# Probabilities stationary in self-attention's value products, Tanh time scales and another startup order in a decoder layer

## The reference, cut to what matters

```python
q_in = linear(x, Wq_w, Wq_b)            # then a width-3 convolution, and a projection of both
Q = linear(concat(q_in, conv1d(q_in)), qproj_w, qproj_b)     # the same for K; V = linear(x)
tau   = sigmoid(conv1d(gelu(conv1d(x, tau1_w)), tau2_w))     # per head and query
delta = sigmoid(conv1d(gelu(conv1d(x, del1_w)), del2_w))     # per head and key
scores = Q @ K.T / sqrt(8) * tau + delta
out = softmax(scores) @ V               # [heads, 128 queries, 8]
x = x + linear(out, out_w, out_b)
```

## Time and profile before

| | |
|---|---|
| median of 3 runs | 305.3 us |
| the profiled execution | 305.65 us, of which 303.8 us from its first to its last instruction |
| PE, ScalarE, VectorE, GpSimd busy | 95%, 63%, 75%, 61% of the span |
| PE weight loads (PEld) busy | 68% of the span |
| mean granted PE clock | 0.987 of full |

### The profile page before, as it was taken

One profiled execution on the slowest core, in us unless ns is written; L12 is line 12 of the kernel. 1 busy time (PEld: TensorE's weight loads), 2 busy tenths in 40 slices (PEclk: granted clock), 3 DMA queues, 4 the chain that ended last, 5 costly groups with the idle time before them and its releaser, 6 DMA issues.

```text
span 303.8 us, 5436 instructions
## 1 busy us (share of the span) xinstructions
PE 288.5 (95%) x1721; PEld 206.5 (68%) x1721; DVE 227.5 (75%) x511; ACT 192.7 (63%) x353; POOL 185.1 (61%) x258
## 2 busy tenths in 40 slices
PE   8999599999999999899879999999999999999995
PEld 3754476667655665466664788888888888888883
DVE  3695599789959886989796559788965766676664
ACT  2787647887784667466752797666655555555553
POOL 8430044087807880876167699999975666666661
PEclk9999789999999999999999999999999999999999
DMA  7703635447477233250000637866444344343321
GB/s 269 230 2 48 204 77 135 109 109 258 110 192 145 62 94 107 62 152 16 0 2 18 185 118 200 216 191 200 122 108 138 112 168 123 128 137 128 118 69 35
DMA packets 30636, 37.18 MB, mean 122 GB/s; under 512 B 5136, under 2 KB 19856, under 8 KB 30608
## 3 DMA queue, kind: packets, MB, share of 16 engines
q1 hardware_dynamic: 30608, 36.84, 43.3%
HBM read 28.43 MB, written 3.93 MB: 107 GB/s over the span
## 4 chain that ended last, share of the span: by engine, by line
PE 79%; DVE 14%; ACT 4%; issue 2%; ACTq 0%; DVEq 0%
PE bank L484 54%; PE bank L863 5%; PE bank L865 5%; PE bank L864 5%; PE bank L669 2%; DVE rawmax L1282 2%; PE bank L644 2%; PE bank L687 2%; DVE conv L1221 2%; DVE conv L1219 2%; PE bank L656 1%; PE bank L692 1%; PE bank L653 1%; PE bank L490 1%; DVE tauT L1349 1%
## 5 line engine op out<-in xcount | busy, mean ns | idle before, releaser
L1846 POOL TENSOR_TENSOR qbd<-vs,qbd 128x512 fp32r<-128x512 f32 x65 | 83.6, 1289 | 33.3 <-ACT qbd L1160 33.2
L484 PE MATMUL bank<-khl,stacks 128*128 128x512 f32 x396 | 101.5, 392 | 1.9 <-DVE vs L1643 1.9
L484 PEld LDWEIGHTS bank<-khl,stacks 128*128 128x128 f32 x396 | 73.5, 188 | 18.7 <-issue 3.7
L1674 DVE TENSOR_TENSOR conv<-bank,conv 128x512 f32<-128x512 f32 x60 | 41.5, 691 | 31.5 <-ACT bank L1124 28.3
L1124 ACT ACTIVATE bank<-bank 128x512 f32<-128x512 f32 x61 | 35.5, 582 | 44.0 <-PE bank L484 44.0
L1282 DVE TENSOR_REDUCE rawmax<-bank 128x4 f32<-128x512 f32 x64 | 43.2, 683 | 8.8 <-PE bank L484 7.8
L484 PE MATMUL bank<-stacks 128*128 128x512 f32 x96 | 42.8, 498 | 4.4 <-DVE stacks L1258 3.3
L1160 ACT ACTIVATE qbd<-vs 128x512 fp32r<-128x512 f32 x65 | 40.6, 625 | 7.1 <-DVE vs L1651 4.6
L1682 DVE TENSOR_TENSOR vs<-conv,bank 128x512 f32<-128x512 f32 x61 | 41.9, 687 | 2.1
L1048 ACT ACTIVATE conv<-bank 128x512 f32<-128x512 f32 x64 | 35.1, 596 | 6.3 <-PE bank L484 5.4
L1810 POOL TENSOR_TENSOR stacks<-ring,stacks 128x384 fp32r<-128x384 f32 x33 | 33.6, 1017 | 1.4
(11 more groups left out here) (238 smaller groups left out, 439.6 us busy)
## 6 DMA issues: line engine op xcount, KB each, us to landing
conv<-coefficient_rows SPq DMA_DIRECT2D x122, 128.0 KB, 2.9
ring<-w SPq DMA_DIRECT2D x33, 192.0 KB, 3.6
stacks<-stacks SPq DMA_DIRECT2D x68, 64.0 KB, 2.1
split_rows<-stacks SPq DMA_DIRECT2D x6, 256.0 KB, 2.6
stacks<-split_rows SPq DMA_DIRECT2D x16, 96.0 KB
split_rows<-khl SPq DMA_DIRECT2D x3, 512.0 KB, 4.3
stacks<-split_rows SPq DMA_DIRECT2D x8, 192.0 KB
pa<-pack_a SPq DMA_DIRECT2D x1, 706.0 KB, 5.4
```

Of the source, the lines that this page charges most:

```text
L484: return pe.matmul(out, lhsT, rhs, start=start, stop=stop)
L1674: dve.tensor_tensor(out, gate, spread[:, n % ROWS, :, :], ALU.mult).then_inc(gate_scaled, 1)
L1846: pool.tensor_tensor(hlo[:, n % 4, :].rearrange("p (b t) -> p b t", b=4), hx[n % 4], hhi[:, n % 4, :].bitcast(F32).rearrange("p (b t) -> p ...
```

## The change

1. Time scales: ScalarE computes Tanh of half the argument, with half the bias (tau_half, made on GpSimd), and VectorE makes the Sigmoid of it, 0.5 t + 0.5, before the query product.
2. Startup order: PE turns the first inputs before it sums the queries' bias, and sums the keys' bias after the first query convolution; ScalarE copies the keys' composed taps after the first tap, and runs the high keys' first half and the first time scales before the last late Gelu; VectorE adds the folded biases between tau's and delta's taps and makes the first low keys before the query products.
3. Value products of self-attention: the probabilities (128 keys x 128 queries) are stationary and the values (128 keys x 9) moving; the result has the queries on partitions and lies in bank 4 as 16 x 9 columns (attended). copy_o and turn_out run for cross-attention alone; norm reads bank 4 directly in self-attention.
4. Query quadrants: in self-attention ScalarE copies all four, VectorE none. Waits follow these changes.

```diff
+        attended = bank[4][:, 0:H * (DK + 1)].rearrange("p (h c) -> p h c", h=H)
...
             compose(0)
+            turn_inputs(0, 0, bank[0])
             sum_bias(0, "qp2T", "cqb", "bq")
-            turn_inputs(0, 0, bank[0])
             compose(1)
-            sum_bias(1, "kp2T", "ckb", "bk")
             turn_inputs(0, 1, bank[1])
...
                 convolve(0, convq, c, bank[5 + c]).then_inc(q_done, 1)
+                if c == 0:
+                    sum_bias(1, "kp2T", "ckb", "bk")
...
             def turn_max(s):
                 wait(pe, qbd_high, s)
-                wait(pe, qbd_ready, s)
+                wait(pe, qbd_ready, s - B)
...
             def pv(s, g):
                 i = G * s + g
                 pe.wait_ge(exped, i + 1)
-                if g == 0:
-                    wait(pe, o_copied, s)
+                if g == 0 and s <= B:
+                    wait(pe, normed, s)
+                elif g == 0:
+                    pe.wait_ge(o_copied, s - B)
                 for j in range(J):
-                    last = mm(bank[4][32 * j:32 * j + DK + 1, P * g:P * g + P], vs[s // B][:, s % B, J * g + j, :],
-                              probs[:, i % 8, j, :])
+                    h = J * g + j
+                    if s < B:
+                        last = mm(attended[:, h, :], probs[:, i % 8, j, :], vs[0][:, s, h, :])
+                    else:
+                        last = mm(bank[4][32 * j:32 * j + DK + 1, P * g:P * g + P], vs[1][:, s % B, h, :], probs[:, i % 8, j, :])
...
             def turn_on(s):
                 pe.wait_ge(normed, s + 1)
+                wait(pe, residual, s)
...
-                if s >= 1 and making is None:
+                if s > B and making is None:
                     turn_out(s - 1)
...
             copy_inputs(0, 0, 0)
-            copy_composed(1, convk)
             copy_inputs(0, 1, 1)
...
+            def time_scales(c):
                 act.wait_ge(tau_done, c + 1)
-                act.activation(half(tauT, c), four(3 + c), ACT.Sigmoid, bias=A("tau2b")).then_inc(tau_ready, 1)
+                act.activation(half(tauT, c), four(3 + c), ACT.Tanh, scale=0.5, bias=tau_half[:, :]).then_inc(tau_ready, 1)
...
+            first_tap(0, 0, "tau1", "tau1b")
+            copy_composed(1, convk)
+            first_tap(0, 1, "tau1", "tau1b")
...
+            first_tap(1, 0, "del1", "del1b")
+            early_gelu(0)
+            first_tap(1, 1, "del1", "del1b")
+            early_gelu(1)
+            fill_keys(1)
+            fill_keys(2)
+            late_gelu(0)
+            fill_keys(3)
             act.wait_ge(bias_folded, 2)
+            act.wait_ge(k_done, 1)
+            high_keys(0, 0, 7, foldb[:, 1:2])
+            act.wait_ge(halves_ready, 2)
+            time_scales(0)
+            late_gelu(1)
+            time_scales(1)
             high_queries(0)
             high_queries(1)
-            act.wait_ge(k_done, 1)
-            high_keys(0, 0, 7, foldb[:, 1:2])
             act.wait_ge(k_done, 2)
             high_keys(0, 1, 0, foldb[:, 1:2])
...
-                for j in range(J - 1 if s < B else 2):
+                for j in range(J if s < B else 2):
...
-                if s >= 1:
+                if s > B:
                     copy_o(s - 1)
...
+            low_keys(0, 0, 7, foldb[:, 1:2])
             for c in range(2):
                 dve.wait_ge(q_done, c + 1)
                 dve.wait_ge(tau_ready, c + 1)
+                dve.tensor_scalar(half(tauT, c), half(tauT, c), 0.5, 0.5, ALU.mult, ALU.add).then_inc(tau_scaled, 1)
+                dve.wait_ge(tau_scaled, c + 1)
...
             low_queries(0, 0)
-            low_keys(0, 0, 7, foldb[:, 1:2])
+            low_keys(0, 1, 0, foldb[:, 1:2])
             low_queries(0, 1)
-            low_keys(0, 1, 0, foldb[:, 1:2])
...
             def norm(s):
-                dve.wait_ge(o_turned, s + 1)
-                o = bank[6][:, :].rearrange("p (h c) -> p h c", h=H)
+                if s < B:
+                    dve.wait_ge(pv_done, G * s + G)
+                else:
+                    dve.wait_ge(o_turned, s - B + 1)
+                o = attended if s < B else bank[6][:, :].rearrange("p (h c) -> p h c", h=H)
...
-                if s < STEPS:
+                if B <= s < STEPS:
                     queries_with_max(s)
```

More of the change, by code:

```diff
@@ L101, in decoder_layer @@
         natural = qin[:, :, :].rearrange("p b t -> p (b t)")[:, 4 * P:6 * P].rearrange("p (n i) -> p n i", n=2)
-        negbias = sb("negbias", [P, 2])
+        small = sb("small", [P, 3])
+        negbias, tau_half = small[:, 0:2], small[:, 2:3]
         foldb = sb("foldb", [P, 2])
@@ L208, in decoder_layer @@
         tau_ready = sem("tau_ready")
+        tau_scaled = sem("tau_scaled")
         delta_done = sem("delta_done")
@@ L664, in scoresT @@
                     pe.wait_ge(qbd_high, s + 1)
-                    pe.wait_ge(qbd_ready, s + 1)
+                    wait(pe, qbd_ready, s - B + 1)
                 wait(pe, exped, i - 1)
@@ L807, in _ @@
                     scoresT(s, 3)
-                if making is not None:
+                if making is not None and s > B:
                     turn_out(s - 1)
@@ L849, in _ @@
             pe.wait_ge(exped, G * STEPS)
-            pe.wait_ge(o_copied, STEPS)
+            pe.wait_ge(o_copied, STEPS - B)
             products(0)
@@ L975, in _, with high_queries, late_gelu @@
             act.wait_ge(ld_a, 16)
[L976 to L990, removed]
+            def high_queries(c):
+                act.wait_ge(q_ready, c + 1)
+                act.activation(half(qhl[:, 0, :, :], c), half(qc, c), ACT.Copy).then_inc(qhi_ready, 1)
+            def late_gelu(r):
                 act.wait_ge(conv_done, 3 + r)
@@ L993, in _, with early_gelu @@
                     act.activation(gelu_half(r, b), conv[:, 2 + r, b:b + 4, :], ACT.Gelu).then_inc(gelu_done, 1)
-            for c in range(2):
+            def early_gelu(r):
+                act.wait_ge(conv_done, r + 1)
+                act.activation(conv[:, r, :, :], conv[:, r, :, :], ACT.Gelu).then_inc(gelu_done, 1)
+            def time_scales(c):
                 act.wait_ge(tau_done, c + 1)
-                act.activation(half(tauT, c), four(3 + c), ACT.Sigmoid, bias=A("tau2b")).then_inc(tau_ready, 1)
-            def high_queries(c):
-                act.wait_ge(q_ready, c + 1)
-                act.activation(half(qhl[:, 0, :, :], c), half(qc, c), ACT.Copy).then_inc(qhi_ready, 1)
-            act.wait_ge(bias_folded, 2)
+                act.activation(half(tauT, c), four(3 + c), ACT.Tanh, scale=0.5, bias=tau_half[:, :]).then_inc(tau_ready, 1)
+            t0 = cols_a["tau2T"][0]
+            act.wait_ge(xT_copied, 2)
+            first_tap(0, 0, "tau1", "tau1b")
+            copy_composed(1, convk)
+            first_tap(0, 1, "tau1", "tau1b")
+            act.activation(tau2r[:, :, :, :].rearrange("p r h d -> p (r h) d"),
+                           pa[:, t0:t0 + 2 * H].unsqueeze(2).broadcast_to([P, 2 * H, DK]), ACT.Copy).then_inc(const_ready, 1)
+            first_tap(1, 0, "del1", "del1b")
[6 more added lines that the diff above has]
+            fill_keys(3)
+            act.wait_ge(bias_folded, 2)
+            act.wait_ge(k_done, 1)
[4 more added lines that the diff above has]
+            time_scales(1)
             high_queries(0)
             high_queries(1)
-            act.wait_ge(k_done, 1)
-            high_keys(0, 0, 7, foldb[:, 1:2])
             act.wait_ge(k_done, 2)
@@ L1034, in copy_o @@
                 act.wait_ge(pv_done, G * s + G)
-                wait(act, o_turned, s)
+                wait(act, o_turned, s - B)
                 act.activation(oT[:, :, :].rearrange("p g t -> p (g t)"), bank[4][:, :], ACT.Copy)\
@@ L1209, in _ @@
             last.then_inc(picks_ready, 1)
-            dve.wait_ge(bias_summed, 2)
-            for n, bias in enumerate(("qpb", "kpb")):
-                dve.tensor_tensor(foldb[:, n:n + 1], bank[4][:, n:n + 1], A(bias), ALU.add).then_inc(bias_folded, 1)
             def later_taps(n, w):
@@ L1226, in _ @@
             later_taps(0, "tau1")
+            dve.wait_ge(bias_summed, 2)
+            for n, bias in enumerate(("qpb", "kpb")):
+                dve.tensor_tensor(foldb[:, n:n + 1], bank[4][:, n:n + 1], A(bias), ALU.add).then_inc(bias_folded, 1)
             later_taps(1, "del1")
@@ L1241, in values, with low_keys @@
                 last.then_inc(v_copied, 1)
+            def low_keys(n, c, b, bias):
+                dve.wait_ge(khi_ready, 2 * n + c + 1)
+                dve.scalar_tensor_tensor(out=half(khl[n][:, 1, :, :], c), in0=four(b), scalar=bias,
+                                         in1=half(khl[n][:, 0, :, :], c).bitcast(F32), op0=ALU.add,
+                                         op1=ALU.subtract).then_inc(klo_ready, 1)
+            low_keys(0, 0, 7, foldb[:, 1:2])
             for c in range(2):
@@ L1295, in queries_with_max @@
                 wait(dve, scoredT, G * (s - 1))
```

(6 more changed lines are left out.)

2 lines of the change are left out of this document (1 added, 1 removed).

## The result

The changed kernel takes 339.94 us, median of 4 runs (338.24 to 343.9), against 305.48 for the kernel before on the same chip: ratio 1.1112 [1.1069, 1.1155]. The forecast was 325.6 with a range of 313 to 334: the direction was right, the size too small by some 14 us, and the time lies outside the range. The profiled execution is the one of 338.24 us.

A forecast was written before the change was run, and what follows sets the result against it. Startup was taken as bound by a VectorE-ScalarE chain, self-attention steps by PE's queue, then exponentials, last maximum and normalisation. Sum: 305.65 - 3.5 (startup) + 16.8 (value products, transposes) + 7 (clock) = 325.95, or 325.6 on the median's footing; range 313 to 334.

The forecast's parts named there:

- the clock: Self-attention steps: about one stretch of PE at half rate in each of seven steps, +7 us, bounds 0 and +13.
- Value products and transposes: Self-attention steps: longer products +2.26 us, removed transposes credited 0.16; +2.1 each step, +16.8 over eight.
- Query quadrants: Self-attention: ScalarE's fourth copy adds 0.60 us, hidden at no cost; with short products it would stand on the path.
- New waits: Self-attention: value products waiting for the previous norm to read bank 4, and turn_on's wait on the residual, cost nothing.
- Startup up to the stacking: Startup: PE starts stacking at 31.4 instead of 33.58, and a full clock shortens its products; startup -3.5 us.
- SP must keep up ... no loss: Startup transfers: eight end at 31.9, six more take 3.08 us to 35.0, when step 1's blocks leave without loss.
- The clock stays full: Rival for the self-attention steps: no half-rate stretches, total 318.95 us (315 to 321); chance 0.22.
- Tanh not under Gelu's table: Rival for the startup: three table loads instead of one, about +2 in place of -3.5, total 331.5 us; chance 0.08.
- Loads beside each other: Rival for value products: 128x128 tile loads overlap, products cost as before, total 298 us; decides from 0.06 us an instruction; chance 0.08.

The follow-up runs named there:

- the keys first: Startup part of the change alone on the kernel before, with SP issuing step 1's keys ahead of the split queries' rows: 301.75 us, ratio 0.9862.
- 63-column run: The changed kernel with each self-attention value product streaming its 9 value columns seven times over, same loads: 320.56 us, ratio 1.0486.

## Why the prediction was wrong, by its own steps

**The step that failed: the clock.** The mechanism was named, and its price was nearly right; how long the clock stays down was wrong. The prediction had "about one stretch at half rate in each of seven steps", each of 3.41 us at 1.0 us apiece, +7. Measured: 17.4 us for 48 us at half rate, that is 14 of the prediction's stretches, at 1.24 us each. The clock did not fall more often than forecast: it was at half six times in the steps, from 54.2, 61.0, 88.3, 95.1, 105.4 and 115.6, for 3.4, 20.5, 3.4, 6.8, 6.8 and 6.8 us. Only those of steps 1 and 4 (54.2 and 88.3) are as short as forecast. In steps 5, 6 and 7 the clock fell already in the second block of value products and came back only with the end of the step. The forecast also assumed that a step's score half would bring the clock back before the next step's products. It didn't always: from within step 2 to the end of step 3 it stayed at half for one stretch of 20.5 us, in which PE was idle for 0.32 us, while the stretch behind it is at full clock:

```profile
61.01:81.49 20.48, 20.16 (x72) 16.67 (x73) 6.75 (x18) 7.40 (x15) 8.91 (x12) 0.50 0.18 41
81.49:88.32 6.83, 6.61 (x50) 5.70 (x49) 3.86 (x12) 3.44 (x6) 2.58 (x13) 1.00 0.70 253
```

The price per stretch was reckoned for the score half, 1.0 us. On the product blocks half rate takes 7.12 us for 3.81. Even the bound of +13 (1.7 us in each of eight steps) allowed one such stretch a step, and so was no bound. What brings the clock down is shown by the runs with 9, 27, 63 and 126 columns behind the same loads: 48, 24, 0 and 0 us at half rate in the steps. At half rate the loads slow down too (3.77 us of them become 7.02 in the product blocks above). Why the clock returns when it does was not tried and stays open. The row that the term was read from the earlier trace rows was thin evidence: with the keys first, the same delta products run at 36.01 and 37.59, and the clock stays full to 49 us.

**Value products and transposes: right as a sum.** 3.81 us was forecast for the block at full clock, and 3.81 measured in step 1. With the clock full throughout, the steps cost 16.5 us more; the forecast was 16.8. Step by step it is less exact: in the 63-column run the steps grew by 1.39 to 2.58 us, where 2.1 was forecast for each. In its step 3 the score half grew by 0.45 us (2.88 to 3.33), where 0.16 was credited for the transposes, so part of the agreement is luck. The delta products, loads of the same tile with 16 columns streamed, were the right row to price it by.

**Query quadrants: right, with its condition.** Hidden in the changed kernel, and at full clock too (in step 3 of the 63-column run the copies end at 67.67, and PE asks for them at 69.25). Without the longer products to hide them, and with copy_o kept, they cost 1.65 us over the eight steps, 1.04 of it in step 3 (5.30 to 6.34) and 0.50 in step 6 (6.09 to 6.59). The prediction's 0.6 for that case is not reached in most steps; in step 3 the copy itself is 0.44.

**New waits: right.** At full clock the 63-column run has no gap before its products. Of the idle time of PE that the trace notes in its steps, most is for the exponentials (1.1 us) and the maxima (1.0), which the kernel before waits for as well (0.3 each); none of it is a new wait.

**Startup up to the stacking: right.** The stacking starts at 31.17, where 31.4 was forecast; the rescaling takes 0.43 (0.42 was taken); at full clock the stacking is 1.21 us shorter (1.3 was forecast). At the last of the key products before the wait the kernel is 3.62 us ahead (38.53 against 42.15), the forecast's 3.5.

**Startup, "SP must keep up ... no loss": wrong, by 2 us.** The prediction put the six split-row transfers down at 3.08 us because they had taken that before. But there SP had been free for 3.13 us ahead of them (from 30.40, the end of the eight, to 33.53); now they follow the eight directly. They took 4.93, and step 1's keys left at 37.32 instead of 35.0. PE's wait of 2.15 us followed, which left 1.75 us of the gain (41.77 against 43.52), and with 6.78 us at half rate (40.57 to 47.35) 1.25 us were left at turn_max(1). Keys first brought them back: 3.88 us at that mark.

With these the sum closes on the profiled execution. To the forecast of 325.95 come 10.36 us for the clock (17.36 for 7) and 2.25 for the startup (1.25 gained for 3.5); 0.25 come off for the steps at full clock and 0.06 for all behind them: 338.25, and 338.24 was measured.

**The rivals.** *The clock stays full* (318.95) fell for the change as made, but is what its 63-column form does: 320.56. *Tanh not under Gelu's table* fell: the Trainium skill (ScalarE: Activation LUTs, "Table sets: the hidden batching unit") gives Gelu's set without tanh, while in this trace Tanh follows Gelu and Gelu follows Tanh at 25.37 to 26.98 without a load. The measurement decides. *Loads beside each other* fell: 0.112 us an instruction (16 in 1.79 us, 50.12 to 51.91) and not 0.06.

## What to carry to other kernels

Which operand is stationary set a product's price here: with 128x128 float probabilities loaded and 9 columns streamed, a step's 32 instructions took 3.58 us, against 1.32 with the 9 columns loaded and the probabilities streamed in four tiles side by side. Where small products must stand behind full loads, read the granted clock before trusting PE's busy share, and try streaming more columns behind the same load: here 63 in place of 9 cost nothing and saved 19 us. It repairs the clock only: the 63-column form is still 4.9% slower than the kernel before, whose loads were short. And when a change brings a stage forward, reorder the queue that feeds it as well, moving one transfer at a time: the fetches of maxima that were moved along with the keys gave back all that the keys had gained.

## What was unexpected

- PE busy 98% of a stretch and yet at half clock for 20.5 us (61.01 to 81.49, 20.16 us busy). It covers all of step 3.
- An instruction of a float product with a 128x128 stationary operand takes some 0.11 us at full clock whether 9, 63 or 126 columns are streamed (16 instructions in 1.93, 1.90 and 1.95 us).
- The same six transfers took SP 3.08 us to issue 3.13 us after eight others, and 4.93 right behind them. With the keys first, the three right behind the eight took 2.82 us and the three later ones 1.52. In the two runs that took four or all of the eight away from in front of them, the first three took 1.30 us. So their place right behind the eight goes with the slow issue; what in it makes them slow was not tried.
